# Down weights, last table pass, POOL's row of scatters and the two ends of the combine moved in a mixture-of-experts kernel

## The reference, cut to what matters

```python
h = einsum('bsi,bio->bso', x, W[id]) + b[id]          # 4 x 256 tokens of 256 numbers
y = silu(h @ sw1) * (h @ sw3) @ sw2                   # shared expert, 352 wide
scores = softmax(h @ gate_w)                          # 8 experts
weights, indices = top_k(scores, 2)
cw = zeros(N, 8).at[arange(N), indices].add(weights)
for e in range(8):                                    # routed experts, 176 wide
    y = y + cw[:, e] * (silu(h @ rw1[e]) * (h @ rw3[e]) @ rw2[e])
out = x + y
```

## Time and profile before

| | us |
|---|---|
| median of three runs | 127.83 |
| the profiled execution | 127.45 |
| its span in the trace | 125.8 |
| PE busy | 105.3 (84%) |
| PE weight loads busy | 85.2 (68%) |
| DVE busy | 62.2 (49%) |
| POOL busy | 46.9 (37%) |
| ACT busy | 45.0 (36%) |

### The profile page before, as it was taken

One profiled execution on the slowest core, in us unless ns is written; L12 is line 12 of the kernel. 1 busy time (PEld: TensorE's weight loads), 2 busy tenths in 40 slices (PEclk: granted clock), 3 DMA queues, 4 the chain that ended last, 5 costly groups with the idle time before them and its releaser, 6 DMA issues.

```text
span 125.8 us, 2009 instructions
## 1 busy us (share of the span) xinstructions
PE 105.3 (84%) x554; PEld 85.2 (68%) x554; DVE 62.2 (49%) x202; ACT 45.0 (36%) x111; POOL 46.9 (37%) x63
## 2 busy tenths in 40 slices
PE   6698999999993990079999999999999996999600
PEld 4477887678882560057777778899998994888400
DVE  1045567899822021004675676455555543126992
ACT  4145676612320161005677563454344432001100
POOL 4450378787740000003335433534435344600520
PEclk9999999999999599657999999999999999999995
DMA  3888999952225589951222332331021210029824
GB/s 92 258 272 257 346 348 372 387 205 83 106 106 134 145 188 222 209 180 56 76 91 77 109 118 85 121 114 42 10 83 39 75 50 0 6 46 376 328 87 163
DMA packets 16593, 19.07 MB, mean 152 GB/s; under 512 B 2323, under 2 KB 13447, under 8 KB 16583
## 3 DMA queue, kind: packets, MB, share of 16 engines
q1 hardware_dynamic: 13158, 12.62, 33.5%
q0 software_dynamic: 1984, 4.46, 10.0%
q10 hardware_dynamic: 1440, 1.86, 4.6%
HBM read 12.64 MB, written 7.21 MB: 158 GB/s over the span
## 4 chain that ended last, share of the span: by engine, by line
PE 53%; DMA 17%; POOL 9%; DVE 7%; issue 7%; SPq 2%; ACT 1%; POOLq 1%; DVEq 0%; ACTq 0%
PE bank L774 35%; DMA raw<-in_L_ffn_rw_dram 11%; POOL rows_by_expert L369 7%; DVE x_area L751 6%; PE bank L786 6%; PE bank L943 4%; PE bank L908 3%; DMA y_area<-_out_by_choice_and_token 3%; DMA rows_by_expert<-h_area,slot 2%; DMA _out_by_choice_and_token<-y_area,dest 2%; SPq L310 1%; PE bank L801 1%; PE bank L804 1%; ACT hT_hi L413 1%; POOL cond_area L267 1%
## 5 line engine op out<-in xcount | busy, mean ns | idle before, releaser
L382 POOL DMA_INDIRECT _out_by_choice_and_token<-y_area,dest x23 | 22.7, 986 | 51.1 <-DVE y_area L716 51.1
L774 PE MATMUL bank<-raw,gT_f 88*128 x92 | 24.9, 393 | 7.9 <-DMA raw<-in_L_ffn_rw_dram 6.8
L774 PEld LDWEIGHTS bank<-raw,gT_f 88*128 88x128 f32 x92 | 17.3, 195 | 12.1 <-issue 9.0
L369 POOL DMA_INDIRECT rows_by_expert<-h_area,slot x16 | 16.2, 1012 | 11.2 <-DVE slot L590 7.1
L480 ACT COPY gT_f<-bank 88x256 f32<-88x256 f32 x23 | 8.5, 369 | 25.9 <-PE bank L943 25.9
L716 DVE COPY y_area<-bank 128x256 f32<-128x256 f32 x23 | 9.8, 425 | 14.7 <-PE bank L774 14.7
L774 PE MATMUL bank<-raw,hsT 128*128 x44 | 17.0, 514 | 0.0
L710 DVE TENSOR_TENSOR y_area<-y_area,bank 128x176 f32<-128x176 f32 x23 | 7.8, 338 | 18.3 <-ACT y_area L476 18.3
L774 PE MATMUL bank<-w_all,hsT_hi 128*128 x48 | 14.4, 343 | 0.0
L476 ACT ACTIVATE y_area<-bank 128x176 f32<-128x176 f32 x23 | 7.3, 318 | 12.0 <-PE bank L774 11.4
L908 PE MATMUL bank<-ident,h_area 128*128 128x128 f32 x46 | 9.4, 287 | 2.0 <-DMA h_area<-rows_by_expert 2.0
(11 more groups left out here) (118 smaller groups left out, 151.4 us busy)
## 6 DMA issues: line engine op xcount, KB each, us to landing
h_area<-rows_by_expert SPq DMA_DIRECT2D x23, 128.0 KB, 2.1
raw<-in_L_ffn_rw_dram SPq DMA_DIRECT2D x16, 176.0 KB
raw<-in_L_ffn_rw_dram SPq DMA_DIRECT2D x2, 704.0 KB
rows_by_expert<-x_area SPq DMA_DIRECT2D x8, 128.0 KB
y_area<-_out_by_choice_and_token SPq DMA_DIRECT2D x4, 256.0 KB, 4.6
y_area<-_out_by_choice_and_token ACTq DMA_DIRECT2D x4, 256.0 KB, 5.2
out_dram<-x_area SPq DMA_DIRECT2D x4, 256.0 KB, 2.0
sh_raw<-in_L_ffn_sw_dram SPq DMA_DIRECT2D x2, 352.0 KB, 5.2
```

The costliest lines, as they stand in the source:

```text
L369: nc.gpsimd.indirect_dma_start(out=rows_dram, out_offset=bass.IndirectOffsetOnAxis(ap=slot[:, i, t:t + 1], axis=0), in_=h_sb[:, t, :], in_ ...
L382: nc.gpsimd.indirect_dma_start(out=y_dram, out_offset=bass.IndirectOffsetOnAxis(ap=dest[:, j:j + 1], axis=0), in_=y_sb[j % NBY], in_offset ...
L774: last = nc.tensor.matmul(dst, w, v, start=start and n == 0, stop=stop and n == len(operands) - 1)
```

## The change

Six things are done.

1. On SP, the two `raw2` transfers and the two `sh2_raw` transfers are issued directly after the filling, ahead of the waits for the starts, for `filled` and for `dispatched`. Tiles 0 to 7 are then loaded in one row.
2. The low part of block 0 leaves POOL. DVE does it after `hT_lo_of(3, 1)` and ahead of `two_highest_of(2)`; POOL's 16 scatters follow each other.
3. On PE, `table()` comes before `turn_rows(0)`.
4. On PE, in step 23 the last tile's gated values are turned ahead of `down(21)`, not behind it.
5. The reads of the first and of the last batch's results are made in two pieces of 128 KB for each choice, with a semaphore each, and DVE combines a piece's row block with both choices before it waits for the next piece.
6. The store of the last batch is made in two pieces, each when its half is ready.

```diff
@@ SP
             for e in range(E):
                 sp.dma_start(rows_dram[e * ROOM:e * ROOM + P, :], x_sb[:, 0, 0, :]).then_inc(filled, 16)
+            for c in range(2):
+                sp.dma_start(raw2[:, :, c, :],
+                             rw2[:, c * FH:(c + 1) * FH, :].rearrange("e p d -> p e d")).then_inc(raw2_in, 16)
+            sp.dma_start(sh2_raw[0:M0, 0, :], sw2[FS - M0:FS, :]).then_inc(sh2_in, 16)
+            sp.dma_start(sh2_raw[:, 1:NSH, :], sw2[0:FS - M0, :].rearrange("(c p) d -> p c d", p=P)).then_inc(sh2_in, 16)
...
             sp.wait_ge(filled, 16 * E)
             sp.wait_ge(dispatched, 16 * TOPK * NT)
-            for j in range(NBH // 2):
+            for j in range(NBH):
                 load_tile(j, first_starts[j])
-            for c in range(2):
-                sp.dma_start(raw2[:, :, c, :],
-                             rw2[:, c * FH:(c + 1) * FH, :].rearrange("e p d -> p e d")).then_inc(raw2_in, 16)
-            for j in range(NBH // 2, NBH):
-                load_tile(j, first_starts[j])
-            sp.dma_start(sh2_raw[0:M0, 0, :], sw2[FS - M0:FS, :]).then_inc(sh2_in, 16)
-            sp.dma_start(sh2_raw[:, 1:NSH, :], sw2[0:FS - M0, :].rearrange("(c p) d -> p c d", p=P)).then_inc(sh2_in, 16)
...
-            for b in range(B):
-                sp.dma_start(y_tok[:, b, 0, :], y_by_choice[0, b]).then_inc(y_in[b], 16)
-            for b in range(B):
+            read_rows(sp, 0)
+            for b in range(B - 1):
                 sp.wait_ge(out_ready, JS * (b + 1))
                 sp.dma_start(out_tiled[b], x_sb[:, b].rearrange("p j d -> p (j d)")).then_inc(out_stored, 16)
+            for j in range(JS):
+                sp.wait_ge(out_ready, JS * (B - 1) + j + 1)
+                sp.dma_start(out_tiled[B - 1][:, j * D:(j + 1) * D], x_sb[:, B - 1, j, :]).then_inc(out_stored, 16)
@@ used by SP and ACT
+        pieces = [JS if b in (0, B - 1) else 1 for b in range(B)]
+        def read_rows(queue, i):
+            for b in range(B):
+                for n in range(pieces[b]):
+                    cols = slice(n * JS * D // pieces[b], (n + 1) * JS * D // pieces[b])
+                    queue.dma_start(y_tok[:, b, i, cols], y_by_choice[i, b][:, cols]).then_inc(y_in[b][n], 16)
@@ POOL
-            dispatch(0)
-            pool.wait_ge(sh_hi_ready, 1)
-            nc.gpsimd.tensor_tensor(sh_lo[:, :, shared_cols(0)], sh_raw[:, :, shared_cols(0)],
-                                    sh_hi[:, :, shared_cols(0)].bitcast(F32), ALU.subtract).then_inc(sh_lo_pool, 1)
-            for b in range(1, B):
+            for b in range(B):
                 dispatch(b)
@@ DVE
             hT_lo_of(3, 1)
+            sh_lo_of(0)
             two_highest_of(2)
...
             for b in range(B):
-                dve.wait_ge(y_in[b], 16 * TOPK)
...
+                for n in range(pieces[b]):
+                    dve.wait_ge(y_in[b][n], 16 * TOPK)
+                    for i in range(TOPK):
+                        for j in range(n * JS // pieces[b], (n + 1) * JS // pieces[b]):
+                            weigh(b, i, j)
@@ PE
+            table()
             turn_rows(0)
-            table()
             for s in range(NTILE + 2):
                 if s + 1 < NTILE:
                     turn_rows(s + 1)
                 if s < NTILE:
                     up(s)
+                if s == NTILE:
+                    turn_gated(s - 1)
                 if 0 <= s - 2:
                     down(s - 2)
-                if 0 <= s - 1 < NTILE:
+                if 0 <= s - 1 < NTILE - 1:
                     turn_gated(s - 1)
```

More of the change, by code:

```diff
@@ L198, in adaln_moe_ffn @@
         scattered = [sem(f"scattered{i}") for i in range(NBY)]
-        y_in = [sem(f"y_in{b}") for b in range(B)]
+        pieces = [JS if b in (0, B - 1) else 1 for b in range(B)]
+        y_in = [[sem(f"y_in{b}_{n}") for n in range(pieces[b])] for b in range(B)]
         out_stored = sem("out_stored")
@@ L216, in adaln_moe_ffn @@
         sh_hi_ready = sem("sh_hi_ready")
-        sh_lo_pool = sem("sh_lo_pool")
-        sh_lo_dve = sem("sh_lo_dve")
+        sh_lo_ready = sem("sh_lo_ready")
         htok_ready = sem("htok_ready")
@@ L329, in _ @@
                 sp.wait_ge(scattered[i], 16 * len(range(i, NTILE, NBY)))
-            for b in range(B):
-                sp.dma_start(y_tok[:, b, 0, :], y_by_choice[0, b]).then_inc(y_in[b], 16)
-            for b in range(B):
+            read_rows(sp, 0)
+            for b in range(B - 1):
                 sp.wait_ge(out_ready, JS * (b + 1))
                 sp.dma_start(out_tiled[b], x_sb[:, b].rearrange("p j d -> p (j d)")).then_inc(out_stored, 16)
-            sp.wait_ge(out_stored, 16 * B)
+            for j in range(JS):
+                sp.wait_ge(out_ready, JS * (B - 1) + j + 1)
+                sp.dma_start(out_tiled[B - 1][:, j * D:(j + 1) * D], x_sb[:, B - 1, j, :]).then_inc(out_stored, 16)
+            sp.wait_ge(out_stored, 16 * (B - 1 + JS))
         @block.gpsimd
@@ L493, in _ @@
                 act.wait_ge(scattered[i], 16 * len(range(i, NTILE, NBY)))
-            for b in range(B):
-                act.dma_start(y_tok[:, b, 1, :], y_by_choice[1, b]).then_inc(y_in[b], 16)
+            read_rows(act, 1)
             for b in range(BH, B):
@@ L594, in sh_lo_of @@
                 dve.wait_ge(sh_hi_ready, c + 1)
-                lo_part(sh_lo[:, :, cols], sh_raw[:, :, cols], sh_hi[:, :, cols]).then_inc(sh_lo_dve, 1)
+                lo_part(sh_lo[:, :, cols], sh_raw[:, :, cols], sh_hi[:, :, cols]).then_inc(sh_lo_ready, 1)
             def at_row_of(first, last):
@@ L738, in _, with weigh @@
                 base_of(b)
+            def weigh(b, i, j):
+                t = JS * b + j
+                if i == 1:
+                    dve.wait_ge(combining, t + 1)
+                nc.vector.scalar_tensor_tensor(
+                    out=x_sb[:, b, j, :], in0=y_tok[:, b, i, j * D:(j + 1) * D],
+                    scalar=weight[:, t, i:i + 1], in1=x_sb[:, b, j, :],
+                    op0=ALU.mult, op1=ALU.add).then_inc(combining if i == 0 else out_ready, 1)
             for b in range(B):
-                dve.wait_ge(y_in[b], 16 * TOPK)
                 if b == 0:
@@ L745, in _ @@
                     dve.wait_ge(late_base_ready, b - BH + 1)
-                for i in range(TOPK):
-                    for j in range(JS):
-                        t = JS * b + j
-                        if i == 1:
-                            dve.wait_ge(combining, JS * b + j + 1)
-                        nc.vector.scalar_tensor_tensor(
-                            out=x_sb[:, b, j, :], in0=y_tok[:, b, i, j * D:(j + 1) * D],
-                            scalar=weight[:, t, i:i + 1], in1=x_sb[:, b, j, :],
-                            op0=ALU.mult, op1=ALU.add).then_inc(combining if i == 0 else out_ready, 1)
+                for n in range(pieces[b]):
[3 more added lines that the diff above has]
+                            weigh(b, i, j)
         @block.tensor
@@ L811, in shared_up @@
                 if w == 0:
-                    if c == 0:
-                        pe.wait_ge(sh_lo_pool, 1)
-                    else:
-                        pe.wait_ge(sh_lo_dve, c)
+                    pe.wait_ge(sh_lo_ready, c + 1)
                 if g < 3:
```

## The result

| | before | after |
|---|---|---|
| median of the runs | 127.8 us (126.64 to 127.92) | 120.0 us (119.6 to 121.39) |
| ratio of the times | | 0.943, 95% interval 0.934 to 0.952 |
| profiled execution: its time, its span | 127.45, 125.8 us | 120.07, 118.4 us |
| mean granted clock in it | | 0.967 |

The change makes the kernel faster, by 7.8 us in the median and 7.4 in the profiled executions, where 12.1 were forecast. The measured 120.0 lies above the range's high end of 118.5. So the direction and the main step hold, and the size does not.

The account below looks back on a forecast made before the run. PE was taken to bound the tiles from 58 us on, with waits for tile 0's rows, for raw2 and at the tail. Gains 6.85 + 2.06 + 0.4 + 1.6 + 0.6 + 0.6 = 12.1 from 127.45 gave 115.3 us, range 113.8 to 118.5.

Parts of the forecast that it names:

- Part 1: PE before and behind down(0): the wait for raw2 goes, 6.85 us, and the slow start behind it, 2.06 us.
- Parts 2 and 3: Moved transfers beside POOL's row scatters: drained at 37.5, last scatter issued 0.92 earlier, first turn of rows gains 0.4 us.
- queue rival: SP's queue not drained when tile 0 is wanted: turned at 41.5, 1.2 later, dip stays; 118.5 us, 18 in 100.
- Part 4: PE ahead of tile 0: table first shortens the idle time, so the start's clock dip goes; 1.6 us gained.
- the first rival: PE's clock dip at the start stays, as tile 0 comes after too long a pause; 116.9 us, 25 in 100.
- Part 5: End of the tiles: last tile's values turned earlier, so the last result scatter starts at 108.6, not 109.2; 0.6 us gained.
- Part 6: First reads in pieces: DVE's combine starts 0.8 sooner and its 16 operations hide what lands later; 0.6 us gained.
- Part 7: Last batch in pieces and its store in two: together 0, ends -0.4 and +0.5 us.

Follow-up runs that it names:

- e1: Kernel before with only the raw2 and sh2_raw transfers moved behind the filling and tiles 0 to 7 in one row; 121.39 us, ratio 0.967 to before's faster runs.
- e2: Changed kernel with the raw2 and sh2_raw transfers put back to their places of before; 130.33 us, ratio 1.053 to before's faster runs.
- e6: Changed kernel, unchanged, run and profiled again; 119.42 us, ratio 0.933 to before.
- e8: Changed kernel with the two sh2_raw transfers behind the loads of tiles 0 to 7, raw2 still in front; 118.3 us (115.86 to 119.26).
- e14: Changed kernel, unchanged, run and profiled once more, in another set than the earlier repeat; 119.54 us, ratio 0.946 to before.
- e7: Changed kernel with each raw2 transfer of 88 partitions split into 80 and 8; 116.84 us, ratio 0.912 to before.
- e15: Changed kernel with raw2 split into 80 and 8 partitions, sh2_raw behind the tile loads and whole reads; 114.83 us, ratio 0.907 to before.
- e16: e15 with 20 matmuls without use between the table and tile 0's turn; 116.51 us, ratio 0.921 to before.
- e18: The kernel of e15 run a second time, in another set; 114.7 us, ratio 0.902 to before.
- e3: Changed kernel with the combine's reads whole; 121.57 us, ratio 0.983 to before's faster runs.
- e4: Changed kernel with 20 matmuls without use between the table and the first turn of rows; 124.28 us, ratio 1.002 to before's faster runs.
- e9: The kernel of e4 run again, in another set; 124.59 us (122.63 to 124.71).
- e10: The kernel of e3 run again, in another set; 121.9 us, ratio 0.983 to before's faster runs.
- e5: Kernel before, unchanged, run and profiled again; 127.44 us, ratio 0.999 to that set's own runs of before.
- e13: Kernel before, unchanged, run and profiled again in another set; 126.75 us, ratio 0.999 to that set's own runs of before.
- e17: Kernel before, unchanged, run and profiled in the last set; 127.12 us, ratio 0.997 to that set's own runs of before.
- sets 1 and 3: Two of five sets of follow-up runs, of four edited kernels each; before fell into two groups, medians 128.66 and 124.38 us.
- e12: e16 with only the first half of raw2 ahead of tile 0, the second behind tile 3; 123.95 us, ratio 1.001 to before's faster runs.

## Why the prediction was wrong in size

**Part 1 (stall, 6.85 and 2.06): right.** The wait is gone from the chain, and the stretch behind `down(0)` is 2.64 shorter where 2.66 was forecast (2.06 from the clock and 0.6 from the last tile). Moving the transfers alone gives a gain (e1); the rest without it shows none (e2, in the set with the standstills).

**Parts 2 and 3 (gain of 0.4 at the first turn): wrong by 2.0 us, the largest error.** POOL's scatters came sooner, 0.41 more than I had worked out. The step that failed is "I take 0.5 for this and the scatters' slower landing". The landing went from 2.40 to 5.35, in other executions 4.35 and 4.04, so the term was 1.6 to 3 us. I had seen that 1.76 MB must pass beside the scatters, and summed it as a drain that ends at 37.5; but the last scatter is itself among what drains last (queues empty by 39.0 and landing at 39.48, or by 38.0 and 38.50), and SP's load of tile 0 waits for it. That the moved transfers do this is shown by e1 and e2. The queue rival had the size (first turn 41.5, measured 41.85, 40.87 and 40.62 in three profiles) and the wrong place: it put the delay on tile 0's load, whose rows were turned 2.16 after its issue, against 2.20 before. That its time came near is partly luck, as it has no cost for the reads.

The rule of the Trainium skill named beside that rival ("DMA: Bandwidth & Descriptors", section "Why a DMA increments its semaphore by 16 and not by 1": 11 engines for 88 partitions) is borne out in part at most. With 88 partitions the DMA share from 28 to 31 us is 0.83 to 1.02 (after, e6, e8, e14); with 80 and 8 it is 1.10 to 1.12 (e7, e15, e16, e18). But the bytes moved in it do not separate the two, 206 to 297 GB/s against 258 to 283. Nor did `raw2` last until 39.4, the estimate by that rule: the queues are empty by 39.0, 38.0 and 38.0 in the three profiles of the changed kernel.

Against e6, the split alone shortens the landing by 0.06 (e7) and the smaller amount alone by 0.6 (e8), both less than the 1.3 by which the changed kernel's own profiles differ; both together bring it back to 2.40 in all three profiles (e15, e16, e18). I read this as a threshold, the queue drained before the last scatter or not. The late scatters of e3, e4, e9 and e10 fit it (issued at 36.87 to 38.48, first tile load 2.61 or 2.62 behind, with everything in front), but no run varies the amount finely enough to place it.

**Part 4 (start clock, 1.6): the first rival held.** The dip stayed in the profiles of after, 6.64 to 6.80 us from the first turn to `down(0)` against 5.40 without it, so 1.2 to 1.4, not 1.6. The step that failed is the reason I gave, that 1.3 us idle in two pieces would not bring it. PE waited 3.26 us ahead of the first turn (2.27 and 1.96 in e6 and e14), not 1.3, as tile 0 was late; but e6 and e7 show that nearly equal idle time (2.27 and 2.14) goes either way, so the reason was not enough even with its own number. That the gain counts at all was right: the dip of before lay under the wait for `raw2` (e5, e13 and e17 had none at the start, and their waits were 7.17, 7.47 and 8.74 in place of 6.85), and I had counted wait and dip together.

**Part 5 (last tile, 0.6): right.** From the start of the turn of tile 21's gated values to the last scatter it takes 4.58 (96.31 to 100.89) where it took 5.18 (104.02 to 109.20). PE's timelines of before and of after have these turns as

```profile
104.02 0.38 PE L943 MATMUL bank<-ident,y_area 128*88 128x128 f32 x2
```

```profile
96.31 0.60 PE L947 MATMUL bank<-ident,y_area 128*88 128x128 f32 x4
97.24 1.99 PE L781 MATMUL bank<-raw,gT_f 88*128 x8 [0.33 <-ACT gT_f L483]
```

so the last two `down` now run in one. POOL's own row sets it, as forecast. This edit was read from the trace and not run alone.

**Part 6 (first reads, 0.6): wrong sign, 1.8 us off.** The first pieces did come sooner (2.8 in place of 3.5). The step that failed is that DVE's 16 operations "hide everything that lands later". The second batch's rows landed late. The rate tells it, in the windows of after and of e15, each just behind the start of the reads' data:

```profile
105.00:107.00 2.00, 2.00 (x11) 1.76 (x10) 1.19 (x4) 0.00 (x0) 0.00 (x0) 1.00 1.00 227
```

```profile
101.10:103.10 2.00, 2.00 (x11) 1.76 (x10) 0.55 (x2) 0.11 (x1) 0.00 (x0) 1.00 1.04 384
```

At a full share, 227 GB/s in place of 384 (376 in the same stretch of before). The pieces read rows half as long, and while they run the queues move about 0.6 of the bytes. That the length of the rows is the reason, and not the greater number of transfers, is not shown. Over all profiles, from the reads' issue to the end of the combine it is 12.58 to 13.17 with pieces (e2, e6, e7, e8, e9, e14 and after), but for one of 11.97 (e4), and 11.84 to 12.20 with whole reads. Before is among the latter. On the mean the pieces cost about 0.8, and the 1.2 of the main pair is at the high end.

**Part 7 (last piece and store, 0): right**, -0.3 by the span's tail.

Together: 2.0 + 1.2 + 1.8 - 0.3 = 4.7, which is the distance from 115.3 to 120.0. e15 has the change without these three faults, and it ran in 114.8. That this is so near to 115.3 is partly luck: it reaches it with 0.35 MB less in front and with no gain from the reads.

## What to carry to other kernels

When a load is moved into the time in which another queue's small transfers are on the critical path, cost the landing of the last of these, not only the drain of the queue: put in front only what the first consumer needs. Here that and a cut of 88 partitions into 80 and 8 together brought the landing back, and neither alone was seen to. Don't cut a read at the end into shorter rows unless the reads behind it have slack; compare GB/s, not the share. And a slow clock that lies under a wait costs nothing until the wait is taken away, so look for it in several profiles before counting it.

## What the hardware showed that I had not expected

- **A scatter's landing is elastic.** POOL's last row scatter took 2.40 us to land in before, at a DMA share of 0.29 from 31 to 36 us, and 4.04 to 5.35 in the changed kernel, at 0.82 to 0.91, while POOL's issue interval stayed even.
- **The clock dip is no function of PE's busy time alone.** 0.83 and 0.82 us of work in 3.10 us, and a granted clock of 0.52 in one and 1.00 in the other. Four profiles of before have it at the start once, the three of after each time. Where PE waited only 0.3 us there (e15, e18), or had the extra matmuls (e16), it did not come.
- **ACT and DVE can stand still for microseconds, in some sets and not in others.** In seven of the eight profiles of sets 1 and 3 one of them or both stood still for "remote", up to 7.53 us, between 20 and 41 us; in the eighth (e9) PE waited 3.29 us there for nothing that is named. No profile of the other sets has such a wait. The Trainium skill ("Runtime: NRT & Kernel Launch", section "Instruction fetch mechanics") says that engines stream their instructions by DMA in blocks of 16 KiB, at a cost "mostly hidden"; that such a fetch waits behind the data is a guess that no run here tests, and the 4.55 us of e2 at a DMA share of 0.24 and the 4.55 us of e12 at 0.32 (up to 37.86) don't speak for it. Each set was on one chip, so whether it belongs to the chip or to the hour is open too. e15 was not run in such a set, so what it brings there is open as well.
